# Three edits to a graph, attention and expert kernel: bank pairs for V, the order of one tile, weights loaded by expert

## What is computed

```python
h = relu(gat(layernorm(x), W1, ...)); x = x + gat(h, W2, ...)      # two graph attention layers
y = layernorm(x)
z = y + attention(layernorm(y) * ln1_g + ln1_b)                    # 12 heads of 64, over all 1250 rows
out = x + z + moe(layernorm(z) * ln2_g + ln2_b)                    # 8 experts, 2 for each row
# gat:  e[i,j] = leaky_relu(e_dst[i] + e_src[j]); softmax over i's neighbours; out_i = sum_j a_ij (h W)_j + b
# moe:  for each row the 2 largest of 8 router logits; expert(r) = gelu(r W1_e) W2_e, weighted by a softmax of the two
```

## Time and profile before

| | us |
|---|---|
| median of 3 runs (1572.43 to 1579.07) | 1574.52 |
| profiled execution, its own time | 1568.86 |
| span of its trace | 1567.1 |
| PE busy in it | 1424.7 (91%) |
| DVE, ACT, POOL busy | 1154.7, 968.8, 508.2 |

### The profile page before, as it was taken

How to read it: one execution, slowest core, us unless ns; L and a number is a source line. 1 busy time by engine, 2 the same in 40 slices (tenths; PEclk the granted TensorE clock), 3 DMA queues, 4 the chain that set the end, 5 groups by cost and what they waited for, 6 DMA issues and landing times.

```text
span 1567.1 us, 25494 instructions
## 1 busy us (share of the span) xinstructions
PE 1424.7 (91%) x8979; PEld 1343.9 (86%) x8979; DVE 1154.7 (74%) x1752; ACT 968.8 (62%) x1656; POOL 508.2 (32%) x365
## 2 busy tenths in 40 slices
PE   3998799999699979999999999999988996799996
PEld 1896488999699979899898998989988996799995
DVE  6788889625779652486868868688687887788884
ACT  7996976522568322366857667576777311788884
POOL 2000000000000001244636446364466310488886
PEclk9999699999799999999999999999999997899998
DMA  7001000221225440000000000000001594699883
GB/s 196 2 1 41 1 10 21 82 85 53 100 64 162 137 149 1 1 21 1 21 0 0 20 0 20 0 0 0 20 22 41 163 282 94 213 251 249 244 231 102
DMA packets 59910, 121.49 MB, mean 78 GB/s; under 512 B 11152, under 2 KB 27156, under 8 KB 59824
## 3 DMA queue, kind: packets, MB, share of 16 engines
q1 hardware_dynamic: 48448, 98.09, 20.0%
q0 software_dynamic: 11376, 22.29, 6.6%
HBM read 89.57 MB, written 44.31 MB: 85 GB/s over the span
## 4 chain that ended last, share of the span: by engine, by line
PE 59%; DVE 10%; DMA 6%; issue 4%; ACT 2%; POOL 2%; ACTq 0%; SPq 0%; POOLq 0%; DVEq 0%
PE ps L368 11%; PE ps L369 11%; PE ps L370 11%; DMA xg<-xg_d,index 4%; PE ps L808 4%; PE ps L849 4%; PE ps L851 3%; PE ps L828 3%; PE ps L850 3%; PE ps L830 3%; DVE mcol L1050 2%; DMA vtin<-xn_d 2%; PE ps L591 1%; DVE prlo L1019 1%; PE ps L817 1%
## 5 line engine op out<-in xcount | busy, mean ns | idle before, releaser
L1019 POOL TENSOR_TENSOR prlo<-prob,prhi 125x500 fp32r<-125x500 f32 x180 | 249.0, 1389 | 273.0 <-ACT prob L961 272.3
L1050 DVE TENSOR_REDUCE mcol<-ps 125x1 f32<-125x1250 f32 x120 | 175.0, 1458 | 78.2 <-PE ps L808 77.6
L959 ACT ACTIVATE prhi<-ps 125x500 fp32r<-125x500 f32 x300 | 177.0, 590 | 74.9 <-PE ps L830 69.4
L849 PE MATMUL ps<-prhi,vhi 125*128 125x250 f32 x600 | 173.1, 288 | 10.4 <-POOL prlo L1019 4.8
L961 ACT ACTIVATE prob<-ps 125x500 f32<-125x500 f32 x300 | 176.4, 588 | 2.1 <-DVE prlo L1019 2.0
L1506 POOL MEMSET q<- 128x2500 f32 x1 | 2.2, 2187 | 532.4 <-PE ps L370 532.4
L851 PE MATMUL ps<-prlo,vhi 125*128 125x250 f32 x600 | 169.2, 282 | 0.0
L850 PE MATMUL ps<-prhi,vlo 125*64 125x250 f32 x600 | 168.2, 280 | 0.0
L1648 PE MATMUL ps<-ohs,ohd 128*125 128x417 bf16 x380 | 124.2, 389 | 39.2 <-DVE ohs L2063 38.6
L828 PE MATMUL ps<-qst,kst 128*125 128x250 f32 x600 | 156.6, 284 | 3.4 <-issue 1.4
L830 PE MATMUL ps<-q,k 128*125 128x250 f32 x600 | 153.7, 280 | 0.0
(11 more groups left out here) (324 smaller groups left out, 4057.8 us busy)
## 6 DMA issues: line engine op xcount, KB each, us to landing
w2st<-in_L_ffn_W_dram SPq DMA_DIRECT2D x27, 1152.0 KB
w1all<-in_L_ffn_W_dram SPq DMA_DIRECT2D x8, 1152.0 KB, 9.3
wqst<-in_L_ffn_Wqkv_dram SPq DMA_DIRECT2D x12, 384.0 KB, 4.3
hid_d<-tin SPq DMA_DIRECT2D x10, 375.0 KB
hin<-hid_d SPq DMA_DIRECT2D x10, 375.0 KB
vtin<-xn_d SPq DMA_DIRECT2D x10, 375.0 KB
out_dram<-accr POOLq DMA_DIRECT2D x10, 375.0 KB, 9.0
xall<-in_x_dram SPq DMA_DIRECT2D x5, 672.0 KB
```

What stands on the lines that cost most here:

```text
L849: pe.matmul(ps[:, b:b + GQ], vhi[:, e, kt, :], hi, start=kt == 0, stop=False)
L959: act.activation(prhi[:, n % RING, :], bank(3 + n % 3, P, 2 * GQ), ACT.Exp, scale=float(HD) ** -0.5)
L1019: eng.tensor_tensor(prlo[:, n % RING, :], prob[:, n % 3, :], prhi[:, n % RING, :].bitcast(f32), ALU.subtract)\
L1050: dve.tensor_reduce(mcol[:, e, t:t + 1], ps[0:P, 0:N], AX.X, ALU.max, negate=True).then_inc(sem("max"), 1)
```

## The change

It has four parts.

1. *V stage.* The turned tiles take the banks 0 and 1 or 2 and 3 by turns, so `v_turn(t)` waits for `v_lower(t - 2)` and no longer for `v_lower(t - 1)`. `vtin` has three buffers with semaphores of their own. On DVE three `v_affine` stand in the last steps of the graph layer where two stood, and later `v_lower(t)` comes ahead of `v_affine(t + 2)`. On ACT `v_higher(2)` moves ahead of the last step's rows. On SP the loads of tiles 0 to 2 go up into the layer, one each, tile 3's load comes after the stores of row tile 8, and tile 4's after those of row tile 9.
2. *Second layer's first tile.* PE makes the first 10 triple sums of tile 0 before it turns tile 1; on DVE `weigh(0)` comes ahead of `leaky(1)` and `lower(0)` ahead of `weigh(1)`, and on ACT `higher(0)` ahead of `exponential(1)`.
3. *Four row buffers.* The gathered rows have four buffers; a fifth gather is issued before POOL's loop, and in the loop tile j + 5 is gathered.
4. *Second weights by expert.* SP loads each expert's second weights once, 8 loads, into the buffer e % 2, as soon as all tiles of expert e - 2 have been split. A new table `eslot` gives the buffer of each tile; `upto` is `cum` + 1. ACT reads two numbers into registers before it splits (buffer and expert), DVE one. DVE makes the two tables in `w2_tables`, four small instructions after the first tile. Tiles with no rows count as expert 7 and no longer as 0.

```diff
@@ v_turn, v_higher, v_lower, v_affine
-            u = t % 2
-            if t == 0:
+            if t < 2:
                 pe.wait_ge(sem("agg_lo"), 2 * T + 1)
             else:
-                pe.wait_ge(sem("tile_lo"), 2 * T + t + 2)
+                pe.wait_ge(sem("tile_lo"), 2 * T + t + 1)
...
-                at = k // 3 * BANK + k % 3 * P
-                last = pe.transpose(ps[:, at:at + P], vtin[:, u, k * 128:(k + 1) * 128], ident[0:P, 0:P])
+                at = (t % 2 * 2 + k // 3) * BANK + k % 3 * P
+                last = pe.transpose(ps[:, at:at + P], vtin[:, t % 3, k * 128:(k + 1) * 128], ident[0:P, 0:P])
@@ agg_pe
             turned(pe, n, 0, 0)
+            sums(0, 0, range(T))
+            turned(pe, n, 1, 1)
+            sums(0, 0, range(T, 2 * T))
             with pe.Fori(0, T // 2 - 1) as i:
-                turned(pe, n, 2 * i + 1, 1)
-                sums(2 * i, 0)
                 turned(pe, n, 2 * i + 2, 0)
                 sums(2 * i + 1, 1)
-            turned(pe, n, T - 1, 1)
-            sums(T - 2, 0)
+                turned(pe, n, 2 * i + 3, 1)
+                sums(2 * i + 2, 0)
@@ sync, V rows
             for t in range(T - 2):
                 g2_rows(t)
-                if t == 3:
-                    v_in(0)
-                    v_in(1)
-            v_in(2)
+                if 3 <= t < 6:
+                    v_in(t - 3)
             g2_rows(T - 2)
             v_in(3)
+            g2_rows(T - 1)
             v_in(4)
-            g2_rows(T - 1)
             v_in(5)
@@ sync, second weights
-            for j in range(TILES):
-                if j >= 2:
-                    sp.wait_ge(sem("w2_lo"), j - 1)
-                e = sp.value_load(etile[0:1, j:j + 1], min_val=0, max_val=NE - 1)
...
+            for e in range(NE):
+                if e >= 1:
+                    sp.wait_ge(sem("w2_in"), 16 * e)
+                if e == 2:
+                    sp.wait_ge(sem("route_dve"), LAST_TILES)
+                if e >= 2:
+                    sp.wait_ge(sem("w2_lo"), sp.value_load(upto[0:1, e - 2:e - 1], min_val=1, max_val=TILES + 1))
+                sp.dma_start(w2st[:, e % 2, :, :], w2.rearrange("e (k r) f -> e r k f", r=128)[e, :, :, :]).then_inc(sem("w2_in"), 16)
@@ gpsimd
             pool.wait_ge(sem("route_dve"), ADDS)
+            gather(4)
             for j in range(TILES):
-                if j + 4 < TILES:
-                    gather(j + 4)
+                if j + 5 < TILES:
+                    gather(j + 5)
                 add_first(j)
                 add_second(j)
@@ scalar, split_w2
-                act.wait_ge(sem(f"w2_in{u}"), 16 * (j // 2 + 1))
+                if j == 0:
+                    act.wait_ge(sem("route_dve"), W2_SLOT)
                 if j >= 2:
                     act.wait_ge(sem("y_raw2"), j - 1)
...
+                s = act.value_load(eslot[0:1, j:j + 1], min_val=0, max_val=1)
+                act.wait_ge(sem("w2_in"), act.value_load(etile[0:1, j:j + 1], min_val=0, max_val=NE - 1) * 16 + 16)
@@ vector, after V
+            v_affine(dve, 3)
             for t in range(2, T):
-                if t + 1 < T:
-                    v_affine(dve, t + 1)
                 v_lower(dve, t)
+                if t + 2 < T:
+                    v_affine(dve, t + 2)
@@ vector, tables
+            def w2_tables():
+                dve.sem_inc(sem("w2_lo"), 1)
+                dve.wait_ge(sem("route_dve"), ADDS)
+                dve.tensor_scalar(upto[:, :], cum, 1.0, None, ALU.add).then_inc(sem("route_dve"), 1)
+                order.did(dve.scalar_tensor_tensor(owner[:, 2, :, :], over_i(ecol[:, 6, :]), -1.0, owner[:, 0, :, :], ALU.add, ALU.mult))
...
```

More of the change, by code:

```diff
@@ L214, in build @@
     wvlo = put("wvlo", [128, KD, D], f32r, at=WVAT)
-    vtin = put("vtin", [P, 2, D], f32, at=put.end)
+    vtin = put("vtin", [P, 3, D], f32, at=put.end)
     lnrow = put("lnrow", [P, 2, D], f32, at=ATT)
@@ L297, in build @@
     xain1 = put("xain1", [P, D], f32, at=max(ATT_END, put.end))
+    xg3 = put("xg3", [S, ROW], f32, at=put.end - 4 * D)
     gslot = put("gslot", [S, TILES], f32, at=put.end)
     gjunk = put("gjunk", [S, 2, NE], f32, at=put.end)
+    upto = put("upto", [S, NE], i32, at=put.end)
+    eslot = put("eslot", [S, TILES], i32, at=put.end)
     w1hi = put("w1hi", [128, 2, KD, FF], f32r, at=XT)
@@ L543, in v_higher @@
             act.activation(xthi[:, :, t * P:(t + 1) * P].rearrange("p (a k) c -> p a k c", a=2),
[L544 removed]
+                           two(t % 2 * 2, 128, 3 * P).rearrange("p a (k c) -> p a k c", k=3), ACT.Copy).then_inc(sem("tile_hi"), 1)
         def v_out(act, t):
@@ L658, in agg_act @@
             for k in range(T + 3):
+                if k == 0:
+                    higher(act, n, 0)
                 if k + 1 < T:
@@ L715, in step @@
             def step(k):
+                if k == 0:
+                    lower(dve, n, 0)
                 if k + 1 < T:
                     weigh(dve, n, k + 1)
-                if k < T:
+                if 0 < k < T:
                     lower(dve, n, k)
@@ L732, in agg_dve @@
             maximum(1)
+            weigh(dve, n, 0)
             leaky(dve, n, 1)
-            weigh(dve, n, 0)
             maximum(2)
@@ L1541, in _ @@
             order.did(pool.memset(ecol[:, 7, :], 1.0))
+            order.did(pool.iota(ecol[:, 6, :].rearrange("p (a b) -> p a b", b=2), [[0, NE // 2], [1, 2]], base=0, channel_multiplier=0,
+                                allow_small_or_imprecise_dtypes=True))
             order.did(pool.affine_select(out=tri[:, :], in_=ones[:, 0:P], compare_op=ALU.is_gt, fill=0.0,
@@ L2409, in weight @@
                                          accum_out=gslot[:, j:j + 1]).then_inc(sem("gslot"), 1)
+            def w2_tables():
[3 more added lines that the diff above has]
+                order.did(dve.scalar_tensor_tensor(owner[:, 2, :, :], over_i(ecol[:, 6, :]), -1.0, owner[:, 0, :, :], ALU.add, ALU.mult))
+                order.wait()
+                order.did(dve.tensor_reduce(pick[:, 0, :], owner[:, 2, :, :], AX.X, ALU.add))
+                order.wait()
+                dve.tensor_scalar(eslot[:, :], pick[:, 0, :], 1.0, None, ALU.add).then_inc(sem("route_dve"), 1)
             split_w1(0)
@@ L2413, in _ @@
             weight(0)
+            w2_tables()
             split_w1(1)
```

68 lines of the change are left out of this document (34 added, 34 removed).

## The result

The changed kernel took 1550.27 us (median; 1549.63 to 1554.04) beside 1573.47 us for the kernel before on the same chip: ratio 0.9853, 95% interval 0.9821 to 0.9885. The profiled execution took 1550.63 us with a span of 1548.9, beside 1568.86 and 1567.1 before: 18.2 us less.

The account below looks back on a forecast made before the run. PE was taken as the bound, busy 1424.7 of 1567.1 us. Gains of 1.4 + 6.5 + 11.7 = 19.6 us gave 1549.3 for the profiled execution and 1555 as median, own range 1548 to 1560, wider range 1547 to 1567.

Parts of the forecast that it names:

- First tile, 1.4 us: Head of the second layer: `weigh(0)` and the turn of tile 0 come earlier, gaining 1.4 us, bounds 0 and 3.
- V stage, 6.5 us: V stage: turn of tile 9 at 581.8 against 588.41, with tile 4 still waiting 6.3 us; gain 6.5 us.
- Waits of the experts, 13.6 us: Experts: fourth buffer and fewer loads remove all gather waits, 24 tiles at 7.27 us each; gain 13.6 us.
- Register loads, 0.7 us for the pace: Experts: register loads before `w2hi` on ACT cost 0.03 us a tile, a loss of 0.7 us, bounds 0 and 7.
- Start and end, 0.7 and 0.5: Experts: tables and second expert's load cost 0.7 us at the start; the last tile's later split costs 0.5.
- DMA share below 0.5: Experts: a sign that the forecast holds, DMA share falling below 0.5 from 0.83 to 0.88.
- The sum: Whole kernel: gains of 1.4, 6.5 and 11.7 make 19.6 us, so the profiled execution would take 1549.3 us.
- 1 (ACT the bound): Experts: register loads cost the full 1.3 us, pace 7.6, 8 us lost, total 1563; chance 0.14.
- 2 (POOL the bound): Experts: the buffer's lead is eaten at 0.5 a tile, 7.3 of 13.6 us come, total 1561; chance 0.08.
- 3: V stage: tile 4's load, or each one, keeps PE waiting; the stage gives 1 us, total 1560; chance 0.10.
- 4 (loads drain the engine): Experts: register loads wait for the instruction ahead, 8.1 to 8.7 us a tile, total 1573 to 1587; chance 0.06.
- 5 (no effect of the graph part): Graph and attention parts: nothing measurable, for instance because what follows absorbs their waits; no chance of its own given.

Follow-up runs that it names:

- rows_4_5_ahead: Changed kernel with the loads of row tiles 4 and 5 put ahead of the stores of row tile 9 in SyncE's queue: median 1551.58 us.
- one_more_load: Changed kernel with one register load more in front of each `w2hi` on ScalarE: median 1556.93 us.
- load_per_tile: Changed kernel with w2 loaded for each of the 27 tiles as before, four row buffers kept: median 1554.71 us, ratio 0.9909 to the kernel before.
- loads_behind_w1hi: Changed kernel with the two register loads of a tile's w2 split put behind ScalarE's w1 split, one round earlier, except the last tile's: median 1550.36 us.
- v_as_before: Changed kernel with the V stage put back (two row buffers, one bank pair, old orders): median 1557.67 us, ratio 0.9919 to the kernel before.
- wqlo_later: Changed kernel with row loads 4 to 7 moved ahead and GpSimd's first query and key weight split behind the last row's scaling: 1542.55 us, ratio 0.9824.

## Why the prediction was right, and where its terms were off

The experts' term was right in mechanism and size, the first tile's nearly so; the V stage's was right about tile 4 and missed what comes behind it.

- **First tile, 1.4 us.** `weigh(0)` and the turn of tile 0 came 1.43 us earlier, as worked out. Undoing the edit alone takes away 1.0 to 1.3 at tile 2. The first sum starts 12.05 us behind the layer's first maximum, where the turn of tile 1 had started at 13.49, and the cover held: PE turned tile 1 with no wait.
- **V stage, 6.5 us; measured 4.1 in this pair.** Tile 2 without wait, tile 3 with 0.2 for 1 us, tile 4 with 7.02 for 6.3: "tile 4's load has been put behind the stores of row tile 9" is shown right by `rows_4_5_ahead`, and the low clock behind it cost 1.8, as worked out (5.62 for 3.8). What the sum did not have is tile 7, which "The later loads have three buffers and run ahead." should have kept free. It cost 1.6 us more than its pace, though its row was there: GpSimd's `wqlo` stretched DVE's `v_affine` to 4.10 us. The later rows ran ahead only because tile 4's wait gave them time. And "If tile 4's load is not late it is 14" was wrong: with tile 4 in time, tile 6 takes over its wait, and the stage gives 4.6 (45.51 less 40.93); with tiles 4 to 7 moved it gives 12 to 13. The turns at full clock are 3.78 to 3.87 apart, not 3.73, and tile 4's load took 8.0 us to land, not 7.2.
- **Waits of the experts, 13.6 us; measured 13.96.** The lead of one loop did it: three buffers leave 7 us of it to be paid, four buffers with the old 27 loads leave none. The 13.96 are 9.0 us of idle time, at most 1.7 of low clock, and some 0.25 for each of 12 waits. My sentence "gathers can only get faster" with fewer loads was wrong where it counts: with 8 loads one of them, at full DMA share, still made a gather 3.4 us late.
- **Register loads, 0.7 us for the pace; measured 0.1.** `w2hi` came 1.23 us behind `xhi`, inside 1.1 to 1.3; the cover of 0.57 took it, with 0.05 left by the row and some 0.2 by `one_more_load`. The Trainium skill (DMA: Bandwidth & Descriptors, Latency and other measured facts) gives about 600 ns as the floor of a register load; here a further load moved `w2hi` by 0.45 us, which is less, and the two loads moved it by nothing where they stood behind a long instruction, so the floor is a latency that the engine can work under.
- **Start and end, 0.7 and 0.5.** At the start -0.40 us in this pair, but two executions of the same kernel differ there by 0.6 (14.68 and 15.31), so it is not told apart from nothing, and `load_per_tile`, which has no tables, has 15.24. At the end the last `htlo` came 1.0 us later than with loads per tile (13.45 against 12.45 behind the last turn), twice my 0.5, since the two loads there cost 0.77 in front of `w2hi`; against the kernel before (12.79) it is 0.7.
- **DMA share below 0.5** was wrong: 0.63 in the long window. I had credited the nineteen loads with too much.
- **The sum**, 1549.3 for the profiled execution, met 1550.63. That is closer than its terms: V gave 2.4 us less than forecast, and the experts, start and end included, 1.1 more (12.85 for 11.7). The forecast of 1555 added the 5.7 us by which the runs shown lay above the profiled one. That difference did not come back: in the later sets of runs the kernel before had medians of 1568.77 to 1570.37, close to its own profiled 1568.86. It belonged to the runs drawn, not to the kernel.
- **Rivals.** 1 (ACT the bound) fell, though by some 0.2 us of slack: `one_more_load` shows it half true one load later. 2 (POOL the bound) fell: the lead of the gathers is 12.7 to 13.1 us from tile 8 to tile 26, no ground is lost. 3 was half true for tile 4. 4 (loads drain the engine) fell by the 1.23 us itself, and by `loads_behind_w1hi`. 5 (no effect of the graph part) fell by `v_as_before`.

Open: what moves the head of the second layer by 1 to 2 us between executions (its first maximum lies between 410.1 and 412.7, whichever order the first layer has), why the granted clock differs between executions of one kernel, what `load_per_tile`'s median holds, and which of `wqlo_later`'s own waits at tiles 6 and 8 could be had back by another order of the loads; none of it was tried.

## What to carry to other kernels

A wait for a transfer is a question of when it was issued against the worst landing, not of how busy the DMA engines are in the mean: one loop of lead covered a share of 0.92, and 27 loads cut to 8, without that lead, still left three waits, one of 3.4 us. When a late load is moved ahead, look at once at the next in the same queue, since the wait moves there whole; moving tiles 4 and 5 gave 0.5 us of the stage, tiles 4 to 7 together 8. Register loads go behind the longest instruction of their engine, one round ahead: here that won back ScalarE's 0.5 us of slack.
